# Moving the seven state exponents of GpSimd to VectorE in a four-layer kernel

## The reference

```python
x_trans = relu(concat(x, lifted) @ Wf1 + bf1) @ Wf2 + bf2
Bm = x_trans @ W2 + b2                     # 16 states per token
Cm = x_trans @ W3 + b3
delta = softplus(x_trans @ W1 + b1)
dB = delta[..., :, None] * Bm[..., None, :]
dA = exp(-celu(delta[..., :, None] * A[None, None]))   # celu(z) = z if z > 0 else exp(z) - 1
h_new = dA * h_prev[:, None] + x_trans[..., None] * dB
output = einsum('bln,bldn->bld', Cm, h_new)
```

## Time and profile before

| what | value |
|---|---|
| three timed runs | 298.43, 300.55, 300.74 us, median 300.55 |
| profiled execution | 299.29 us, of which the span 297.6 us |
| PE busy | 238.8 us, 80% |
| DVE busy | 251.4 us, 84% |
| ACT busy | 178.7 us, 60% |
| POOL busy | 170.5 us, 57% |
| mean granted TensorE clock | 0.924 of full |

### The profile page before, as it was taken

One profiled execution on the slowest core, in us unless ns is written; L12 is line 12 of the kernel. 1 busy time (PEld: TensorE's weight loads), 2 busy tenths in 40 slices (PEclk: granted clock), 3 DMA queues, 4 the chain that ended last, 5 costly groups with the idle time before them and its releaser, 6 DMA issues.

```text
span 297.6 us, 2655 instructions
## 1 busy us (share of the span) xinstructions
PE 238.8 (80%) x825; PEld 155.6 (52%) x825; DVE 251.4 (84%) x358; ACT 178.7 (60%) x234; POOL 170.5 (57%) x121
## 2 busy tenths in 40 slices
PE   1846899696977485975997977979899999999980
PEld 0845567233744143432553443527688877888860
DVE  4996999999997999999899999566995459799455
ACT  3556885576769967576687795175533365173330
POOL 2360888527777337999789885333874227535310
PEclk9989799999999659798699798897999999999997
DMA  6920000000000000000000000000000000020002
GB/s 185 388 88 1 3 0 0 0 1 0 0 2 0 0 0 1 0 2 0 0 0 0 0 1 0 0 2 2 0 2 0 0 0 3 0 70 2 0 0 70
DMA packets 3822, 6.15 MB, mean 21 GB/s; under 512 B 384, under 2 KB 2656, under 8 KB 3552
## 3 DMA queue, kind: packets, MB, share of 16 engines
q1 hardware_dynamic: 3808, 5.97, 5.8%
HBM read 4.92 MB, written 1.05 MB: 20 GB/s over the span
## 4 chain that ended last, share of the span: by engine, by line
DVE 44%; PE 40%; issue 8%; ACT 4%; DMA 1%; POOL 1%; DVEq 0%; ACTq 0%
PE ps L1107 12%; PE ps L1108 12%; PE ps L1078 6%; DVE bs L827 5%; PE ps L1059 4%; DVE bx L827 3%; DVE tr L745 3%; DVE bx L821 3%; DVE bs L821 3%; DVE x1r L745 3%; DVE bs L858 2%; DVE low_max L736 2%; DVE xr L873 2%; DVE tr L747 1%; PE ps L971 1%
## 5 line engine op out<-in xcount | busy, mean ns | idle before, releaser
L599 ACT ACTIVATE bs<-ps,vec 128x512 f32<-128x512 f32 x48 | 32.4, 689 | 38.3 <-PE ps L1108 37.1
L1059 PE MATMUL ps<-tr,h0sel 96*128 96x512 f32 x64 | 23.4, 493 | 14.3 <-DVE bx L827 7.6
L1059 PEld LDWEIGHTS ps<-tr,h0sel 96*128 96x128 f32 x64 | 13.3, 223 | 29.4 <-DVE bs L827 13.9
L1078 PE MATMUL ps<-bs,centre 128*128 128x512 f32 x52 | 28.0, 680 | 0.0
L821 DVE SCALAR_TENSOR_TENSOR bs<-bdl,amax,bs 128x1024 f32<-128x1024 f32 x14 | 26.6, 1929 | 0.0
L1107 PE MATMUL ps<-xr,wf 128*128 128x512 f32 x64 | 25.2, 393 | 0.0
L1108 PE MATMUL ps<-xr,wf 128*128 128x512 f32 x64 | 25.1, 391 | 0.0
L418 POOL TENSOR_TENSOR xr<-bs,xr 128x512 fp32r<-128x512 f32 x12 | 15.9, 1328 | 13.8 <-DVE xr L873 13.8
L567 ACT ACTIVATE bs<-bs 128x2048 f32<-128x2048 f32 x9 | 17.2, 1906 | 10.5 <-DVE bs L821 7.0
L390 POOL TENSOR_TENSOR bxt<-bdl,amax 128x1024 f32<-128x1024 f32 x7 | 18.9, 2702 | 7.4 <-PE ps L1068 6.9
L418 POOL TENSOR_TENSOR tr<-bs,tr 128x512 fp32r<-128x512 f32 x8 | 10.9, 1360 | 18.5 <-DVE tr L873 18.5
(11 more groups left out here) (225 smaller groups left out, 710.5 us busy)
## 6 DMA issues: line engine op xcount, KB each, us to landing
bs<-in_w_mlp_dram SPq DMA_DIRECT2D x2, 1024.0 KB, 9.6
bx<-in_x_dram SPq DMA_DIRECT2D x4, 256.0 KB, 4.5
out_dram<-bdl SPq DMA_DIRECT2D x4, 256.0 KB, 2.3
bx<-in_w_mlp_dram SPq DMA_DIRECT2D x1, 768.0 KB, 7.0
bdl<-in_w_ssm_dram SPq DMA_DIRECT2D x1, 448.0 KB, 9.5
wa<-in_w_attn_dram SPq DMA_DIRECT2D x1, 256.0 KB, 2.7
w0raw<-in_w_ffn_dram SPq DMA_DIRECT2D x1, 192.0 KB, 8.7
h0T<-in_state_dram SPq DMA_DIRECT2D x1, 48.0 KB, 8.9
```

Of the source, the lines that this page charges most:

```text
L599: a.activation(hbuf[k][:, o, :], ps[:, mbank(i, stage, k, o) % RING, :], ACT.Gelu if stage else ACT.Silu, scale=vec[:, s + o:s + o + 1]).t ...
L1059: last = m.matmul(ps[:, 2 * j + k, :], h0sel[:, n, :], tr[0:96, 0, cs(2 * (e // NG) + k)], start=True, stop=True)
L1078: last = m.matmul(ps[:, 4 + 2 * (e // NG) + k, :], centre[:, :], vbuf[e % NB][:, j, k * CH:(k + 1) * CH], start=False, stop=(e % NG == NG ...
```

## The change

All 32 v are made on VectorE. GpSimd's z products and adds go, with their buffer name `zmax`, their semaphores and the rule `v_on_pool`; its eight pairwise sums stay. ScalarE's dA waits for VectorE's count alone. GpSimd's wait for e_first goes with the z products.

```diff
-        zmax = bxt[:, 0:2 * CH]
...
-        def v_on_pool(e, j):
-
-            return e % 2 == 1 and e > 1 and j == 1
...
-            pool.wait_ge(a_ok, 2)
-            pool.wait_ge(e_first, 2)
-            on_pool = [(e, j, n) for e in range(NE) for j, n in enumerate(group_states(e)) if v_on_pool(e, j)]
-
-            def z_product(r):
-
-                e, j, n = on_pool[r]
-                if r:
-                    pool.wait_ge(e_vp, r)
-                g.tensor_tensor(zmax, bdl[:, pair_tokens(e)], amax[:, n:n + 1].broadcast_to([P, 2 * CH]),
-                                ALU.mult).then_inc(e_zp, 1)
-
-            z_product(0)
-            r = 0
             for e in range(1, NE, 2):
-                if r < len(on_pool) and on_pool[r][0] == e:
-                    _, j, n = on_pool[r]
-                    pool.wait_ge(e_zp, r + 1)
-                    pool.wait_ge(e_t, GN * e + j + 1)
-                    g.tensor_tensor(vbuf[e % NB][:, j, :], vbuf[e % NB][:, j, :], zmax, ALU.add).then_inc(e_vp, 1)
-                    r += 1
-                    if r < len(on_pool):
-                        z_product(r)
                 pool.wait_ge(e_p, e)
                 b = vbuf[(e - 1) % NB]
                 g.tensor_tensor(b[:, 0, :], b[:, 0, :], b[:, 1, :], ALU.add).then_inc(e_add, 1)
...
             def state_da(e):
-                on_pool = sum(v_on_pool(h, j) for h in range(e + 1) for j in range(GN))
-                act.wait_ge(e_v, (e + 1) * GN - on_pool)
-                if on_pool:
-                    act.wait_ge(e_vp, on_pool)
+                act.wait_ge(e_v, (e + 1) * GN)
...
             def state_v(e):
                 for j, n in enumerate(group_states(e)):
-                    if not v_on_pool(e, j):
-                        dve.wait_ge(e_t, GN * e + j + 1)
-                        v.scalar_tensor_tensor(vbuf[e % NB][:, j, :], bdl[:, pair_tokens(e)], amax[:, n:n + 1],
-                                               vbuf[e % NB][:, j, :], ALU.mult, ALU.add).then_inc(e_v, 1)
+                    dve.wait_ge(e_t, GN * e + j + 1)
+                    v.scalar_tensor_tensor(vbuf[e % NB][:, j, :], bdl[:, pair_tokens(e)], amax[:, n:n + 1],
+                                           vbuf[e % NB][:, j, :], ALU.mult, ALU.add).then_inc(e_v, 1)
```

More of the change, by code:

```diff
@@ L178, in build @@
             sem(n) for n in ("c_mm", "c_hi", "c_lo", "b_ok", "bc_ok", "bc_mm", "g_ok", "o2_ok")]
-        e_first, e_t, e_v, e_zp, e_vp, e_da, e_ch, e_p, e_add, e_add_last, e_sum = [
-            sem(n) for n in ("e_first", "e_t", "e_v_dve", "e_z_pool", "e_v_pool", "e_da", "e_ch", "e_p", "e_add",
+        e_first, e_t, e_v, e_da, e_ch, e_p, e_add, e_add_last, e_sum = [
+            sem(n) for n in ("e_first", "e_t", "e_v_dve", "e_da", "e_ch", "e_p", "e_add",
                              "e_add_last", "e_sum")]
```

## The result

The changed kernel takes 305.36 us (median of four runs, 304.03 to 306.47), the kernel before 299.94 (298.43 to 300.74, four runs): a ratio of 1.0185 with a 95% interval of 1.0122 to 1.0248. It is slower, by 5.4 us where 5.5 were forecast. The profiled execution took 304.03 us with a span of 302.3, which is 4.7 us more than the one of before.

The account below looks back on a forecast made before the run. VectorE was taken to bound the state stage, with the port it shares with GpSimd as full. Terms 8.4 - 1.85 - 0.5 - 0.5 = + 5.5 us on 299.9 gave 305.4 us, range 301 to 309.5.

Parts of the forecast that it names:

- Seven v at 1.20, + 8.4: State stage, VectorE: one added v in each odd group from e = 3 to 15, 1.20 us each, + 8.4.
- TensorE's waits covered, - 1.85, and - 0.5 of overlap: State stage, VectorE: added v cover six waits for TensorE, - 1.85 us; six 0.08 us instruction overlaps, - 0.5.
- Stalls, - 0.5: State stage: VectorE's v stalled by GpSimd 14.8 us instead of 15.3, since the sums stay; new stall at e = 2.
- The stage: The state stage, between about 105 and 192 us, the only part the change touches; total forecast + 5.5 us.
- A steady period: State stage: two groups of states, one even e and one odd; forecast to grow by 0.96 us.
- The tail, taken as 0, with - 0.7 as its end: After the stage: last C·h stays in low clock, 0; at full clock it takes 1.2 us, - 0.7.
- relieved port: State stage: sums run beside p, so 14.6 us of VectorE stalls go, giving 290.8 us; chance 0.09.
- exclusive time of a period: State stage, two groups: time v and GpSimd tensor_tensor instructions exclude each other, counted 10.1 us before, 7.2 after.
- TensorE as the bound: State stage: lower clock makes p wait 1.04 us for TensorE in each of seven periods, 312.7 us; chance 0.08.

Follow-up runs that it names:

- after_again: The changed kernel unaltered, run again on another chip as a base: 303.15 us, 1.0165 of the kernel before; three of four runs lie between 302.39 and 303.61.
- before_late_sum: The kernel before, with each pairwise sum on GpSimd also waiting for VectorE's v of the next even group: 294.51 us, ratio 0.9869.
- experiment 1: The changed kernel, with each pairwise sum on GpSimd also waiting for both v of the next even group: 292.68 us, 0.9793 of the kernel before.
- experiment 3: The changed kernel with the eight pairwise sums moved from GpSimd to VectorE: 298.50 us, 0.9983 of the kernel before.
- z_kept: The changed kernel plus seven z products on GpSimd that nobody reads, each behind a sum; first sum waits for e_first: 304.62 us, ratio 1.0162.

## Why the prediction was right

Point by point, from the profiled executions:

- *Seven v at 1.20, + 8.4:* all odd pairs stand at 2.47. As forecast.
- *TensorE's waits covered, - 1.85, and - 0.5 of overlap:* the six waits are gone, and what is left is 1.8 us in two, 0.4 and 1.36. As forecast.
- *Stalls, - 0.5:* six even pairs at 4.56 to 4.59, and the new stall at e = 2 is 4.21 - 2.46 = 1.75 instead of 1.85. In sum 14.7 instead of 14.8, so - 0.6.
- *The stage:* from the first p to p of e = 14 it took 184.05 - 109.55 = 74.50 us before and 189.56 - 109.74 = 79.82 after, + 5.32, for a sum of 5.5. A steady period grew by 11.27 - 10.34 = 0.93, for a forecast of 0.96.
- *The tail, taken as 0, with - 0.7 as its end:* the end came true. From p of e = 14 to the last p it takes 193.20 - 189.56 = 3.64 us against 4.31, - 0.67. In the profile of after_again the last C·h also takes 1.20. I had argued that longer pauses of TensorE would keep the slow stretch in the same place; it moved onto matmuls that nobody waits for. Mis-sized by 0.7. Whether the 1.87 us belongs to the kernel before or to its one profiled execution stays open: in all eight other profiles, that of before_late_sum too, the last C·h takes 1.19 or 1.20.

That makes + 4.7 us for the profiled pair, and the medians differ by 5.4. The hit to a tenth of a microsecond is luck within runs that lie 2.4 us apart; experiment 5 puts the same difference at 3.6, or 3.1 by its three close runs. What held is the mechanism, and the runs separate it from its rivals. The relieved port is refuted for this kernel, since the exclusive time of a period fell from 10.1 to 7.2 us by the prediction's count and the even pairs did not move. But as a mechanism it was half right: its condition, the sum beside p, was only missing a wait (experiment 1: 292.7, where the rival said 290.8). TensorE as the bound did not show: its waits fell to 1.8 us, and its 5.29 us for eight matmuls at 181.65 cost VectorE nothing.

The warning of "Perfetto Trace Analysis", section "Optimizing Scalar/DVE Operations", in the Trainium skill, that offloading between these two engines might not help, is borne out for the sums as long as they run early: 303 to 305 us with them on GpSimd, 298.5 with them on VectorE (experiment 3). Released late, they do help there: 292.7 (experiment 1). For the sums, where the work lies in time decides it.

## What to carry to other kernels

When an engine's instruction is longer than its twin elsewhere in the same trace, it may be waiting inside (or, on TensorE, running at a lower granted clock, as the 1.87 us against 1.19 of C·h): subtract the twin's length before you believe a busy share, and look which instruction of the other engine ends where it goes on. Count a moved instruction at its full length on the bounding engine, and a relieved engine at zero until you have found which of its instructions actually blocks; here it was the one that stayed. And try to delay a helper's work to where its partner reads PSUM before moving it anywhere: one added wait was worth 4.3 us to the kernel before (298.85 to 294.51) and some 12 to the changed one.

## What the runs showed of the hardware

- When a VectorE v ended with another v next in line and a GpSimd sum waiting, GpSimd went first in every steady even pair: four of four in the trace of before (4.58 or 4.59 us), six of six in the changed kernel's (4.56 to 4.59 us). At e = 2 the sum already ran, and the first v waited for it (4.21 us).
- A z product with a broadcast second input takes 1.89 us free of v (118.64 in the profile of z_kept, 131.93 in that of before), a sum of the same size with two full inputs 2.36 to 2.38; on VectorE the sum takes 1.21.
- A GpSimd tensor_tensor beside p (one input in PSUM) leaves both at their own length: 2.37 and 2.27 us in experiment 1.
